# A six-stage transformer kernel: finer order of steps in its two attention stages, and PSUM banks dealt by a fuller clock

## The reference, cut to what matters

```python
x = x + 0.5 * ffn0(layernorm(x))      # f0: hidden 1536, weights rounded to fp8
x = x + attn0(layernorm(x))           # a0: 16 query heads, 4 key/value heads, rope, biases
x = x + 0.5 * ffn0(layernorm(x))      # f0
x = x + 0.5 * ffn1(layernorm(x))      # f1: hidden 2048
x = x + attn1(layernorm(x))           # a1: 16 heads, no bias
x = x + 0.5 * ffn1(layernorm(x))      # f1
```

```python
att = where(causal, q @ k.T / sqrt(32), -inf)     # 1024 x 1024
y = softmax(att) @ v
out = concat(y) @ Wo (+ bo)
```

## Time and profile before

| | us |
|---|---|
| three runs | 2558.61, 2565.97, 2567.2; median 2565.97 |
| the profiled execution | 2561.6 |
| its span, first to last instruction | 2559.9 |
| attention loop of a0, first to last `key` | about 341 to 762 |
| attention loop of a1 | about 1589 to 2047 |

### The profile page before, as it was taken

The page is one execution under the profiler, slowest core; times in us unless marked ns, Lnnn a source line. Parts: engine busy times, 40 slices in busy tenths (PEclk is TensorE's granted clock), DMA queues, the critical chain, the costliest instruction groups (busy, mean ns, idle before and its releaser), DMA issues.

```text
span 2559.9 us, 45686 instructions
## 1 busy us (share of the span) xinstructions
PE 2451.0 (96%) x16544; PEld 1938.2 (76%) x16544; DVE 1751.9 (68%) x3608; ACT 1285.7 (50%) x2521; POOL 1509.2 (59%) x2045
## 2 busy tenths in 40 slices
PE   6999989999999999899999999999999889999999
PEld 4788767676768888688888888776777578888887
DVE  7788579979976344756565555788588866565555
ACT  6555346646664223554555443566466645454443
POOL 5433567667662334876677643666456876676662
PEclk9999999999999999999999999999999999999999
DMA  4222032122221110111111113233233211111112
GB/s 152 74 75 71 33 82 52 47 68 56 56 57 50 38 54 1 39 61 50 50 50 50 50 41 75 72 89 73 53 89 86 58 54 50 50 50 56 59 60 74
DMA packets 85840, 154.01 MB, mean 60 GB/s; under 512 B 17264, under 2 KB 26480, under 8 KB 85616
## 3 DMA queue, kind: packets, MB, share of 16 engines
q1 hardware_dynamic: 85616, 151.09, 20.5%
HBM read 87.58 MB, written 13.63 MB: 40 GB/s over the span
## 4 chain that ended last, share of the span: by engine, by line
PE 81%; DVE 6%; POOL 3%; ACT 2%; issue 2%; DMA 1%; SPq 1%; DVEq 0%; POOLq 0%; ACTq 0%
PE psum L1393 41%; PE psum L1444 23%; PE psum L1539 5%; PE psum L1502 5%; PE psum L1520 4%; PE psum L1550 2%; DVE psum L1972 2%; PE psum L1402 1%; ACT s4a1e L1757 1%; DVE s1a0rden L2011 1%; SPq L2251 1%; POOL s1a0e L2166 1%; ACT s1a0e L1757 1%; POOL s4a1e L2166 0%; POOL x L2174 0%
## 5 line engine op out<-in xcount | busy, mean ns | idle before, releaser
L1972 DVE CUSTOM_DVE_ANT_0 psum<-psum,mask_q 128x512 f32<-128x512 f32 (+5 forms) x768 | 413.1, 574 | 97.8 <-PE psum L1502 94.8
L1925 DVE SCALAR_TENSOR_TENSOR x<-psum,x 128x512 f32<-128x512 f32 x256 | 176.7, 691 | 289.6 <-PE psum L1393 289.2
L1757 ACT ACTIVATE s4a1e<-psum,p_scale 128x384 f32<-128x384 f32 (+5 forms) x384 | 206.1, 580 | 93.2 <-PE psum L1520 89.6
L1757 ACT ACTIVATE s1a0e<-psum,p_scale 128x384 f32<-128x384 f32 (+5 forms) x384 | 202.4, 578 | 79.7 <-PE psum L1520 78.3
L1393 PE MATMUL psum<-s5f1wd,s5f1a 128*128 128x512 f32 x768 | 196.7, 393 | 3.0 <-DVE s5f1a L1917 2.2
L1444 PE MATMUL psum<-s3f1h,wmem 128*128 128x512 f32 x768 | 195.3, 397 | 3.4 <-DVE s3f1h L1886 2.2
L1393 PE MATMUL psum<-s3f1wd,s3f1a 128*128 128x512 f32 x768 | 198.1, 393 | 0.3 <-issue 0.3
L1444 PE MATMUL psum<-s5f1h,wmem 128*128 128x512 f32 x768 | 192.6, 394 | 0.0
L2166 POOL TENSOR_TENSOR s4a1e<-s4a1e 128x896 f32<-128x896 f32 (+3 forms) x128 | 164.8, 1287 | 17.5 <-ACT s4a1e L1757 6.6
L2166 POOL TENSOR_TENSOR s1a0e<-s1a0e 128x896 f32<-128x896 f32 (+3 forms) x128 | 164.5, 1285 | 17.1 <-ACT s1a0e L1757 5.8
L1444 PEld LDWEIGHTS psum<-s3f1h,wmem 128*128 128x128 f32 x768 | 143.4, 188 | 38.0 <-issue 4.6
(11 more groups left out here) (233 smaller groups left out, 6186.5 us busy)
## 6 DMA issues: line engine op xcount, KB each, us to landing
raw<-in_down SPq DMA_DIRECT2D x76, 256.0 KB, 3.9
s1a0qst<-s1a0qs SPq DMA_DIRECT2D x96, 128.0 KB, 2.4
s4a1qst<-s4a1qs SPq DMA_DIRECT2D x96, 128.0 KB, 2.4
s4a1kst<-s4a1ks SPq DMA_DIRECT2D x96, 128.0 KB, 2.4
s3f1graw<-in_gate SPq DMA_DIRECT2D x32, 256.0 KB, 3.0
s3f1graw<-in_up SPq DMA_DIRECT2D x32, 256.0 KB, 3.1
s5f1graw<-in_gate SPq DMA_DIRECT2D x32, 256.0 KB, 3.0
s5f1graw<-in_up SPq DMA_DIRECT2D x32, 256.0 KB, 3.0
```

Of the source, the lines that this page charges most:

```text
L1757: act.activation(T[s]["e32"][:, begin_ + z * pw:begin_ + (z + 1) * pw - skip], src, ACT.Exp, bias=p_scale[:]).then_inc(sem["exp"], 1)
L1925: dve.scalar_tensor_tensor(x[:, tile, :], src, 0.5, x[:, tile, :], ALU.mult, ALU.add).then_inc(sem["x_add"], 1)
L1972: dve.tensor_tensor_reduce(scores, scores, mask_q[:, first:first + pw], -1.0, -MASKED, ALU.add, ALU.min, T[s]["negmax"][n % 2][:, column:c ...
```

## The change

The constants become a frozen dataclass `Timing` with one table for a0 and one for a1. A string of tokens gives the order of steps in an even and in an odd unit: S ticks the side jobs, R and r plan the first and second row piece, K and k the first and second key piece, M the mask, A the pair's sum, V two tiles of `pv`, v one tile, B the jobs that start here, T the stacks. The clock in `Pace` gets a hop of 0.12 us for every dependency, more of the dependencies (`not_before`), SP's queue, and other lengths; `bank_turns` and `Pace` are called with the turns of the buffer `e`. The computation is the same, with the same instructions but for the order, the banks and the waits.

```diff
-AHEAD = 13
-FIRST_ROW, LAST_ROW = -AHEAD % ST, (ST - 1 - AHEAD) % ST
-PIECES_AT = 2
-Y_AT = 1
-Y_WAIT = 2
-YT_AT = 2
-O_LAG = 1
-QK_W_AT = 17
-O_W_AT = 23
-NORMS_FROM = 11
-NORM_STEP = 3
-LN_AFTER = (0, 3, 6, 7, 8)
-PIECE_AFTER = {"a0": (1, 1, 2), "a1": (1, 1, 2)}
-PIECE_STEP = 2
-PIECES_LATER = 0
-M_AFTER = (2, 2, 3)
-X_AFTER = 1
-O_STEP = 1
-STACKS_AT = (18, 20, 26, 31)
-PV_LAG = 9
+TIMING = {
+    "a0": Timing(ahead=13, unit=("STRrBKvkM", "KBkSRrMATv"), pv_lag=9, pieces_at=0, pieces_later=0,
+                 piece_step=2, piece_after=(1, 1, 2), qk_w_at=21, stacks_at=(17, 24, 27, 31),
+                 m_after=(2, 2, 3), y_at=0, y_wait=4, yt_at=1, o_w_at=28, o_lag=2, o_step=1, x_after=1,
+                 norms_from=3, norm_step=4, ln_after=(0, 4, 6, 7, 8), values_at=(-6, 4)),
+    "a1": Timing(ahead=13, unit=("RBKTMrkSv", "KBMkTSARvr"), pv_lag=7, pieces_at=0, pieces_later=0,
+                 piece_step=2, piece_after=(1, 1, 2), qk_w_at=11, stacks_at=(19, 20, 25, 31),
+                 m_after=(3, 3, 4), y_at=2, y_wait=3, yt_at=0, o_w_at=25, o_lag=3, o_step=1, x_after=1,
+                 norms_from=3, norm_step=2, ln_after=(0, 13, 16, 17, 19), values_at=(-5, 1)),
+}
...
-            side.tick(0)
-            row_unit(u + AHEAD)
-            for z in range(1 if SEQ - i * P <= CH else 2):
-                plan.append(("key", s, n, i, z))
-            plan.append(("e_mask", s, n, i))
-            if i % 2:
-                plan.append(("e_add", s, n, i // 2))
-            behind.append((n, i))
-            if len(behind) > PV_LAG and i % 2 == 1:
-                times_v(*behind.pop(0))
-                times_v(*behind.pop(0))
-            for job in beside.pop(u, []):
-                side.start(job)
-            if g + 1 < GROUPS_ALL:
-                for j, when in enumerate(STACKS_AT):
-                    if at == when:
-                        for m in names_of_group(s, g + 1):
-                            plan.append(("stack", s, g + 1, m, j))
+            keys = 1 if SEQ - i * P <= CH else 2
+            for token in tm.unit[i % 2]:
+                if token == "S":
+                    side.tick(0)
+                elif token in "Rr":
+                    row_unit(u + tm.ahead, "Rr".index(token))
+                elif token == "K":
+                    plan.append(("key", s, n, i, 0))
+                    behind.append((n, i))
+                elif token == "k" and keys > 1:
+                    plan.append(("key", s, n, i, 1))
+                elif token == "M":
+                    plan.append(("e_mask", s, n, i))
+                elif token == "A":
+                    plan.append(("e_add", s, n, i // 2))
+                elif token in "Vv" and len(behind) > tm.pv_lag:
+                    for unit in behind[:2 if token == "V" else 1]:
+                        times_v(*unit)
+                        behind.remove(unit)
+                elif token == "B":
+                    for job in beside.pop(u, []):
+                        side.start(job)
+                elif token == "T" and g + 1 < GROUPS_ALL:
+                    for j, when in enumerate(tm.stacks_at):
+                        if at == when:
+                            for m in names_of_group(s, g + 1):
+                                plan.append(("stack", s, g + 1, m, j))
...
+HOP = 0.12
...
     def work(self, engine, length, *needs):
-        begin = max([self.free[engine]] + [self.done[n] for n in needs])
+        begin = max([self.free[engine]] + [self.done[n] + HOP for n in (*needs, *self.also)])
+        self.also = []
         self.free[engine] = end = begin + length
         return end
...
+        self.also = self.not_before(*step)
...
-            done[step] = work("pe", cols / 2250 + 0.02, ("m_in", s, where[0]), *banks)
-            done[step] = work("act", cols / 1230 + 0.26, step)
+            cols, width = (cols, width) if cols <= CH else (cols // 2, width // 2)
+            before = self.strips_before[s, where[0], where[1]]
+            done[step] = work("pe", cols / 2250, ("m_in", s, where[0]), *banks)
+            done[step] = work("act", width / 1200 + 0.15, step,
+                              *([("pv", s, before[1], before[2] | 1)] if before else []))
+            done["strip", s, where[0], where[1]] = done[step]
...
-        elif kind in ("pv", "den"):
-            width = SEQ - where[1] * P * (1 + (kind == "den"))
-            done[step] = work("pe", width / 2400 + 0.1,
-                              ("key", s, *where, 0 if width <= CH else 1),
+        elif kind == "pv":
+            done[step] = work("pe", (SEQ - where[1] * P) / 2400 + 0.07,
                               ("sum", s, where[0], where[1] // 2), *banks)
+        elif kind == "den":
+            done[step] = work("pe", (SEQ - 2 * where[1] * P) / 2400 + 0.08,
+                              ("sum", s, where[0], where[1]))
```

More of the change, by code:

```diff
@@ L2 @@
 from contextlib import ExitStack
+from dataclasses import dataclass
 import numpy as np
@@ L122, in into_heads, with first_row, last_row @@
     return s + 1 < len(STAGES) and not is_ffn(s + 1)
+@dataclass(frozen=True)
+class Timing:
+    ahead: int
+    unit: tuple
+    pv_lag: int
+    pieces_at: int
+    pieces_later: int
+    piece_step: int
+    piece_after: tuple
+    qk_w_at: int
+    stacks_at: tuple
+    m_after: tuple
+    y_at: int
+    y_wait: int
+    yt_at: int
+    o_w_at: int
+    o_lag: int
+    o_step: int
+    x_after: int
+    norms_from: int
+    norm_step: int
+    ln_after: tuple
+    values_at: tuple
+TIMING = {
[8 more added lines that the diff above has]
+}
+def first_row(s):
+    return -TIMING[STAGES[s]].ahead % ST
+def last_row(s):
+    return (ST - 1 - TIMING[STAGES[s]].ahead) % ST
 def row_pieces(t):
@@ L407, in group_jobs, with row_unit @@
                     for i in range(4) for n in names_of_group(s, g)]
-        def row_unit(u):
+        def row_unit(u, z):
             n, i = divmod(u, ST)
             if n < HEADS_ALL:
-                t = (u - AHEAD) % ST
-                for z in range(row_pieces(t)):
+                t = (u - tm.ahead) % ST
+                if z < row_pieces(t):
                     plan.append(("row", s, n, t, z))
-                if i == ST - 1:
+                if i == ST - 1 and z == row_pieces(t) - 1:
                     plan.append(("row_min", s, n))
-                    side.start(timed((M_AFTER[0], ("m_tp", s, n)), (M_AFTER[1], ("m_hi", s, n)),
-                                     (M_AFTER[2], ("m_lo", s, n))))
+                    side.start(timed((tm.m_after[0], ("m_tp", s, n)), (tm.m_after[1], ("m_hi", s, n)),
+                                     (tm.m_after[2], ("m_lo", s, n))))
         def values(b):
@@ L444, in attention @@
         tiles, wait = len(side.waiting), 2
-        for u in range(-wait, AHEAD):
-            side.tick((u + wait) * tiles // (AHEAD + wait)
-                      - (u + wait - 1) * tiles // (AHEAD + wait))
+        for u in range(-wait, tm.ahead):
+            side.tick((u + wait) * tiles // (tm.ahead + wait)
+                      - (u + wait - 1) * tiles // (tm.ahead + wait))
             if u >= 0:
-                row_unit(u)
+                row_unit(u, 0)
+                row_unit(u, 1)
             if u % 2 == 0:
@@ L773, in run @@
                               ("sum", s, where[0], where[1] // 2), *banks)
+        elif kind == "den":
+            done[step] = work("pe", (SEQ - 2 * where[1] * P) / 2400 + 0.08,
+                              ("sum", s, where[0], where[1]))
         elif kind == "y_fin":
-            done[step] = work("dve", 0.9, ("pv", s, where[0], ST - 1))
+            done[step] = work("dve", 2.2, ("pv", s, where[0], ST - 1))
+        elif kind == "y_move":
+            done["moved", s, where[0]] = work("sp", 2.6, ("y_fin", s, where[0])) + 1.65
@@ L776, in run @@
         elif kind == "y_hi":
-            done[step] = work("act", 1.1, ("y_fin", s, (where[0] + 1) * HPG - 1))
+            done[step] = work("act", 1.0, ("moved", s, (where[0] + 1) * HPG - 1))
         elif kind == "y_lo":
-            done["yT", s, where[0]] = done[step] = work("dve", 1.2, ("y_hi", s, where[0]))
+            done[step] = work("dve", 1.2, ("y_hi",) + step[1:])
         elif kind == "oproj":
-            done[step] = work("pe", 0.7, ("yT", s, where[0]), *banks)
+            done[step] = work("pe", 0.69, ("y_lo", s, where[0]), *banks)
@@ L782, in run @@
         elif kind == "x_sum":
-            done[step] = work("dve", 0.69, ("oproj",) + step[1:])
+            done[step] = work("dve", 0.62, ("oproj",) + step[1:])
+        elif kind == "bias_x":
+            done[step] = work("pool", 1.25)
         return done[step]
```

163 lines of the change are left out of this document (124 added, 39 removed).

## The result

The changed kernel takes 2591.62 us (median of 4 runs, 2585.0 to 2597.03) against 2566.59 before (4 runs): ratio 1.0102, 95% interval 1.0083 to 1.012. It is slower by 25 us. The forecast was 2574, slower, in a range of 2542 to 2606: 8 us over the median before, a third of what came. The traced execution of the changed kernel took 2585.0 us, 6.6 under its median; that of the kernel before took 2561.6, 5.0 under its own.

The account below looks back on a forecast made before the run. TensorE, busy 96% of the span, was taken to bound the kernel. Full groups +14, looser groups −4 and later maxima +1 gave +11 us on 2561.6, 2572.6, forecast as 2574 us after the run median; range 2542 to 2606.

Parts of the forecast that it names:

- cost 1: Attention loops: 248 added blocks of narrow matmuls at 0.24 us each, 59.5 us of TensorE time, bounds 0 and 99.
- The gain: Attention loops: finer order removes part of 93 us of waits for ACT, DVE or POOL; net +14 and −4 us.
- seven full groups: Groups with TensorE under 2 us idle: each pays 3.8 us for blocks, regains 1.8 of waits; +14 us in all.
- the nine others: Looser groups and the filling: 72 us of waits, 34 us paid for blocks, 38 us of waits gone; −4 us.
- cost 2c: a1: `m_tp` to `m_lo` about one unit later, so maxima reach SP later; +1 us, bounds 0 and 50.
- 2b: PSUM banks dealt anew by a clock with dependencies; in the FFN stages 0 us, bounds −3 and +3.
- B: Rival: the finer order removes most waits, 59.5 of 93 us to break even; 2540 us with 85% gone; chance 0.28.
- C: Rival: switches and waits cancel, mostly absorbed where TensorE waits; within 3 us of 2562 to 2566; chance 0.18.
- D: Rival: a1's maxima reach SP late, +25 us on 28 heads beyond the forecast, 2598 us; chance 0.07.
- Signs: What the trace would show, such as twice the `pv` entries and plain groups lengthening 49 to 51, 53 to 55 us.
- One sign: Forecast called wrong if a lone `pv` can be entered at under 0.1 us.

Follow-up runs that it names:

- experiment 2: Kernel before with one `pv` per unit instead of two per odd unit, and `O_W_AT` 25 for 23: 2614.88 us, ratio 1.0197.
- experiment 1: Changed kernel with the weighted sums in pairs again (V in odd units, no v), all else kept: 2578.28 us, ratio 1.0059.
- Experiments 7: Changed kernel with pairs back and the `ahead`, lags and side jobs of before, new unit order and clock kept: 2609.43 us, ratio 1.0168.
- 8b: Changed kernel with pairs, tables and lags of before, but `m_after` (3, 3, 4) in a1 alone, (2, 2, 3) in a0: 2575.33 us, ratio 1.0051.
- experiment 4: Changed kernel with the old `Pace` and `bank_turns`, so only banks and their waits differ: 2591.76 us, ratio 1.0102.
- experiment 3: Kernel before with the new `Pace` and `bank_turns` alone, so only PSUM banks and their waits differ: 2559.77 us, ratio 0.9976.
- experiment 9: Kernel before with the new clock and `pv` in blocks of four tiles every fourth unit instead of two every second: 2629.49 us, ratio 1.0248.
- experiment 6: Changed kernel with the unit order of before and a1's first stack at unit 16 instead of 19: 2579.64 us, ratio 1.0057.

## Why the prediction was right

It was right in direction and in its range, and it named the cost that experiment 2 shows. Its size was not right: +8 us over the median before, where +25 came. It had given "slower" a chance of 0.45, so the direction was no sure call.

**The blocks (cost 1): right.** 0.24 us a block, whatever it holds, twice as many of them, 59.5 us. The split alone in the old order (+49 us with 13.6 us of waits less) shows it by itself. The rule of the Trainium skill (TensorEngine Tiling (Array Packing), Key Properties), that a change of tiling mode drains TensorE, agrees in form: the price comes with each change of mode and not with the tile's size, 0.24 us for a lone `pv` of 160 columns as for a full block.

**The gain: right in sign, too large.** I let 51 of 93 us of waits go (1.8 in each of seven full groups, 38 in the rest); 35.9 went, and 57.4 stayed where I had said 40 to 50. The term that failed is the full groups'. From the first `key` of a group to that of the next, the seven grew by 3.2, 3.2 (a0: 48.4 to 51.6, twice), 4.7, 3.4, 3.8, 4.0 and 3.0 us (a1), in sum 25.5 against the +14 forecast; the nine others came to about −1.5 against −4. That is 11 of the 12 us by which the measured +23 exceeds the forecast +11.

The step under that term was that a named wait taken from a full group is time gained. I had put the seven groups' named waits at 21 us; in the trace they are 28.5, and 18.7 after the change. All of the 9.8 us that went are in a1's five groups, and these grew by 19.0 us, as much as 5 × 16 × 0.24 = 19.2 with nothing given back. a0's two groups kept their named waits (3.4 us each) and grew by 3.2 each, less than 3.8. Nor is all of a1's growth the price of blocks. Its plain group had grown by 3.1 us with the blocks of before (experiment 1), the split adding 1.6; in the old order the split alone adds 5.1 to the same group. What lengthens a full group of a1 in the new order is open. One trace of it is that the weight loads of `row` in a1 wait without a named engine for 5.1 us before and 18.7 us after; they do so too in experiment 1 (18.1) and in experiment 2 (16.5), so either part alone brings that wait.

So the sum "switches added, waits given back" describes one way through the table, from the old order by the split (+49) to the new order (−23). By the other way the new order gives nothing back: it costs 13 us first, and the split 13 more. The forecast has no term for this.

**The maxima (cost 2c): right for this kernel.** I took +1; the wait of `key` went from 1.7 to 0.8 us:

```profile
PE psum L1662 <- DMA s4a1qst<-s4a1mrow: 0.8, 1, 0.8
```

The later `m_after` has another worth, which I had not looked at. Experiments 7 and 8b show it: with the old number in the new a1 string, `m_tp` waits 26.5 us for VectorE's last maxima, and the later number takes 34 us off the time.

**Banks (2b): right to take 0 here,** by experiment 4, and by what lies outside the loops, which changed by 0.5 us; in the old order they give 6 us, which I had not expected. (The group of matmuls from which I took the bounds of the FFN stages, 195.3 us, is not the costliest but the third; the two above it idle 0.3 and 3.0 us, so the bounds stand.)

**Rivals.** B (the order removes most waits) needed 59.5 us and got 36. C is out by the interval. D did not occur. The range's upper end of 2606 has no sum behind it; D's own was 2598.

**Signs.** Plain groups became longer, 49 to 52 and 53 to 57 instead of 51 and 55. One sign was badly put: a lone `pv` is entered at 0.09 us, under the 0.1 that was to prove me wrong, and so was a block in the earlier trace rows. The price to watch is in and out, 0.24.

What I had not thought of: the parts depend on each other. With pairs and the new clock, new units and new tables stand at 2578, old units with new tables at 2580 once their one misplaced stack is mended, new units with old tables at 2575 once a1's `m_after` is; both old are at 2560 (2566 with the old clock). So neither half alone holds the 18 us between 2560 and 2578, and why the new order with pairs waits more (115 us against 78) stays open.

## What to carry to other kernels

Count changes between narrow and wide matmuls as one does instructions, and price them from start to start in a full stretch; a planner's clock that charges a fixed sum per step, as this one does, sees no difference between split and whole blocks. Don't take named waits for time: here 9.8 us of them went from full groups that paid the whole price all the same, and 15 us of them were worth 6 us in experiment 3. Check a sum by stage and by group, since two misses of 10 us had cancelled in the total. When two changes come together, run both kernels between: the split cost 49 us in one order and 13 in the other. An order string and its start numbers are one object: either half with the other's numbers stood at 2611 and 2609 us, one misplaced wait in each costing 32 and 34 us, so a number moves with the token that it counts from.

## What the runs showed of the hardware

The clock fell behind long waits. In experiment 9 TensorE was granted 0.95 of its full level over a0's loop, in the changed kernel, which is never idle long there, 1.00 (0.98 before). Three windows of experiment 9, neighbours:

```profile
372.00:376.00 4.00, 3.02 (x51) 1.85 (x51) 3.02 (x11) 0.78 (x2) 3.68 (x9) 1.00 0.30 70
376.00:379.00 3.00, 0.00 (x0) 0.00 (x0) 1.12 (x1) 1.57 (x3) 1.91 (x2) 0.71 0.97 237
379.00:384.00 5.00, 4.95 (x50) 4.14 (x54) 2.94 (x11) 2.35 (x5) 3.53 (x7) 0.50 0.26 46
```

TensorE was busy 3.02 of the first 4 us and not at all in the next 3 us, and the granted clock there is 0.71: part of it at the lower of the two levels, 1.2 instead of 2.4 GHz. In the 5 us after that it is at work again, and all of them are at the lower level. A long wait is thus paid a second time by the work behind it: in experiment 6 a wait shorter by 20 us gave 32 us of time, with a1's clock at 0.99 instead of 0.97, which over its 491 us is some 10 us (an estimate from the clocks of the two loops). Over a0's 421 us, 0.98 against 1.00 is worth at most some 8 us, by the same estimate; over the whole span 0.993 against 0.995 is worth some 5. But the sum of the waits does not tell the clock: experiment 3 has fewer named waits in a0 than the kernel before (43.8 us against 51.4) and a lower clock there (0.97 against 0.98).

A bank planner's clock, with not one instruction changed, gave 0.24% in one order and nothing in the other.
